# Three early loads of transposed x moved up the load queue, and the first scan's row copies issued by another engine

## The chip, the cores and the metric

The kernel runs on one core of one Trainium2 chip. The metric is the device time of one launch in microseconds (us); the time before is the median of three runs. The core has five engines that each work through a program of their own and wait for one another by semaphores: PE (TensorE, matmuls; PEld are its weight loads), DVE (VectorE), ACT (ScalarE), POOL (GpSimd) and SP (SyncE, which here issues every transfer). Transfers run on 16 DMA engines beside the compute engines.

## The reference, cut to what matters

Layer 0 is an attention over the 4096 pixels of each of four images, layer 1 a binarised 3x3 convolution with a batch norm.

```python
# x: (4, 256, 64, 64); K = 16
xf = x.reshape(B, C, N)                                   # N = 4096
f = einsum('kc,bcn->bkn', w1, xf) + b1[None, :, None]     # 16 features per pixel
energy = einsum('bkn,bkm->bnm', f, f)
attention = softmax(energy, axis=-1)
out = einsum('bcm,bnm->bcn', xf, attention)
x = x + out * 0.1
# layer 1
y = conv3x3(binary_act(x), alpha * sign(weights))
x = (y - mean(y)) * rsqrt(var(y) + eps) * gamma + beta + x
```

## The kernel before

**Tiling.** The attention goes over 32 chunks `t` of 512 columns (eight per image) and, in each, 16 steps `g`. A step makes one 128x1024 piece of energies on PE (line 401), its exponentials on ACT (line 508, tile P), a rounded copy on POOL (line 750, Ph), the remainder on DVE (line 610, Pl) and 24 matmuls on PE that multiply Ph and Pl with the halves xh and xl of the transposed x (line 428). Two steps ahead go the energies, and 24 steps ahead (`LAG`) a scan: it computes all energies of a chunk once in advance to find each row's maximum (DVE, line 600, tile nb) and the sum of its exponentials (ACT, line 519). All engines walk the same list `steps`, which begins 24 steps before the first attention step; `u = n + LAG` numbers the scan units from 0. The first 22 units are wide (128x1024, `scan_wide`, line 418) and go round three PSUM buffers in turn.

**The head.** Before the first scan unit, image 0 must give its features f. Eight pieces of x (512 KB each, `load_piece`, line 249) come in through six buffers; pieces 6 and 7 wait until the matmuls of `project(0)` have read pieces 0 and 1. `project(s)` (lines 392 to 395) turns two pieces into 1024 columns of f, ACT copies them out with the bias (`copy_f`, line 535), DVE splits them in a high and a low part (`split_f`, lines 585 and 593, tile hl). From hl, small copies inside the on-chip memory place the rows:

- `f_rows(s)` (line 272) makes four copies of 100 KB into T, first two for the scan (semaphore `ts_in`), then two for the energies (`te_in`).
- `scan_rows(t)` (line 290) makes three copies of 32 KB into U[t % 2] (semaphore `us_in`), the moving side of chunk t's scan; chunks 0 and 1 take their rows straight from hl[0].

The first scan unit waits for `us_in[0]` at 48 and for `ts_in[0]` at 32. `project(0)`, `(1)`, `(2)` stand ahead of unit 0 in PE's program, `project(3)` ahead of unit 4. On DVE, `split_f(0)` and `(1)` stand ahead of unit 0, `split_f(2)` ahead of unit 2 and `split_f(3)` ahead of unit 4. `split_f(2)` overwrites hl[0] and so waits for `us_in[0]`, `us_in[1]`, `ts_in[0]` and `te_in[0]` in front of line 593.

**The transposed x.** `load_xt(m)` (line 255) loads 512 KB of transposed x into one of three buffers (`XB = 3`, views of the tile wk). POOL makes xh and xl from it, two pairs of instructions for each load (`lower_x`, lines 741 and 743); image 0 has eight loads and so 16 pairs, and they stand ahead of the first `round_p` (line 750) in POOL's program. From the fourth load on, `load_xt` waits for the buffer.

**Order on SP.** All transfers are issued by SP in the order of its program: weights, pieces 0 to 5, pieces 6 and 7, `scan_rows(0)`, `f_rows(0)`, `scan_rows(1)`, then `f_rows(1)`, `load_xt(0)`, `f_rows(2)`, `load_xt(1)`, `f_rows(3)`, `load_xt(2)`, then `load_res(0)` (x for the final sum, line 262), and in the loop `energy_rows(0)` (line 297, a copy from U to U) and the loads 3 to 7 of the transposed x.

After the attention comes the convolution (lines 797 to 1062), which the change does not touch.

Of the kernel before, what the change touches and what calls it, by code (L numbers as in the profile page):

```python
# [6 lines left out]
F32 = mybir.dt.float32  # L7
# [11 lines left out]
KF = 16  # L19
KE = 3 * KF  # L20
KS = KE + 2
S0 = 64
# [14 lines left out]
FU = N // (2 * FW)  # L37
XP = 6
XB = 3
# [53 lines left out]
def attention(nc, x, xt, w1r, cols, wn, wt, rd, x2d, T0, shared):  # L93
# [5 lines left out]
    with ExitStack() as ctx:  # L99
# [10 lines left out]
        U = [sb(f"U{k}", [128, QC], F32R) for k in range(2)]  # L110
# [133 lines left out]
        def _(sp):  # L244
            def load_piece(s):
                if s >= XP:
                    sp.wait_ge(f_filled, 2 * ((s - XP) // 2 + 1))
                b, sl = divmod(s, SL)
                sp.dma_start(xp[s % XP], xb[b, :, :, sl * 512:(sl + 1) * 512]).then_inc(xp_in[s % XP], 16)

            def load_xt(m):
                if m >= XB:
                    sp.wait_ge(xl_done, 2 * (m - XB + 1))
                at = m * (4 * 128 * C)
                sp.dma_start(landed[m % XB].rearrange("p k c -> p (k c)"),
                             xt[at:at + 4 * 128 * C].rearrange("(p n) -> p n", p=128)).then_inc(xt_in[m % XB], 16)
# [18 lines left out]
            def scan_rows(t):  # L275
                b, q = divmod(t, CH)
                s = b * FU + q // 2
                if t < 2:
                    sp.wait_ge(hl_done, 1)
                else:  # L280
                    sp.wait_ge(ts_in[s % 2], 32 * (s // 2 + 1))
                if t >= 2:
                    sp.wait_ge(s_done, unit_count(SU * (t - 1) - 1))
                    sp.wait_ge(ue_in[t % 2], 16 * (t // 2))
                if t < 2:
                    src, row, s = hl[0], t * S0, slice(0, QC)
                else:
                    src, row, s = T[b % 2].bitcast(F32), S0, slice(q * QC, (q + 1) * QC)
                for to, at in ((0, 0), (1, 2), (2, 1)):
                    sp.dma_start(U[t % 2][S0 + to * KF:S0 + (to + 1) * KF, :].bitcast(F32),  # L290
                                 src[row + at * KF:row + (at + 1) * KF, s]).then_inc(us_in[t % 2], 16)
# [34 lines left out]
            sp.dma_start(col[:], cols).then_inc(col_in, 16)  # L326
            for s in range(2, XP):
                load_piece(s)
            for s in range(XP, SL):
                load_piece(s)  # L330
            scan_rows(0)
            f_rows(0)
            scan_rows(1)
            for s in range(1, FU):
                f_rows(s)
                load_xt(s - 1)
            load_res(0)
            for t in range(-1, NT):
                b, q = divmod(t, CH)
# [162 lines left out]
        @block.scalar  # L502
        def _(act):
            def exps(e):
                act.wait_ge(e_done, e + 1)
                if e >= 2:
                    act.wait_ge(pl_done, e - 1)
                mm = nc.scalar.activation(P[:, e % 2, :], ee[:], ACT.Exp)  # L508
                if e < PA:
                    mm.then_inc(p_done, 1)  # L510
                else:
                    act.wait_ge(av_done, 2 * (e - RP + 1))
                    nc.scalar.activation(Ph[:, e % RP, :], ee[:], ACT.Exp).then_inc(p_done, 1)  # L513

            def block_sum(v, to):
                t, j, i = unit_at(v)
                w = j * QT + i
                act.wait_ge(nmax_done, unit_count(v))
                nc.scalar.activation(to, to, ACT.Exp, bias=nb[:, t % 2, w:w + 1],  # L519
                                     accum_out=bsum[:, t % 2, w:w + 1]).then_inc(bsum_done, 1)  # L520

            def copy_bottom(t, c):
                if c == 0:
                    act.wait_ge(acc_done, 2 * (t + 1))
                else:
                    act.wait_ge(av_done, 2 * G * (t + 1))
                if t > 0:
                    act.wait_ge(x2_done, CT * (t - 1) + c + 1)
                nc.scalar.copy(tb[:, c, :], acc_b[c][:]).then_inc(bot_done, 1)  # L529

            def copy_f(s, bank):
                act.wait_ge(f_filled, 2 * (s + 1))
                if s >= 2:
                    act.wait_ge(hl_done, s - 1)
                nc.scalar.activation(Fp[s % 2][0:S0 + KS, :], bank[0:S0 + KS, 0:512], ACT.Identity,
                                     bias=col[0:S0 + KS, 0:1]).then_inc(fp_done, 1)

            act.wait_ge(fill_done, 1)
            nc.scalar.activation(dd[:, 0:1], sr[:, 31:32], ACT.Exp)
            act.wait_ge(col_in, 16)  # L540
            for t, g in steps:
                n = t * G + g
                e, u = n + 2, n + LAG
                for s in HEAD_F.get(u, ()):
                    copy_f(s, acc_t[s % 2])
                if g == 0 and t >= 1:
                    copy_bottom(t - 1, 1)
                if 0 <= e < NG:
                    exps(e)
                if u < UH:  # L550
                    block_sum(2 * u, wide[u % 3][:])
                elif u < NG:
                    block_sum(2 * u, sc[0])
                if g == G - 1 and 0 <= t < NT - 1:
                    copy_bottom(t, 0)
                if UH <= u < NG:
                    block_sum(2 * u + 1, sc[1])
                if g == 8 and 0 <= t + 1 < NT:
                    act.wait_ge(dd_done, t + 2)
                    nc.scalar.activation(wg[:], dd[:], ACT.Exp).then_inc(wg_done, 1)  # L560
                if projected(t, g) is not None:
                    copy_f(projected(t, g), ee)
                h = split_at(t, g)
                if h is not None:
                    m, p = divmod(h, 2)
                    b, k = divmod(h, 2 * XG)
                    act.wait_ge(xt_in[m % XB], 16 * (m // XB + 1))
                    act.wait_ge(av_done, 2 * ((b * CH - 1) * G + k + 1))
                    nc.scalar.copy(xh[:, 2 * k:2 * k + 2, :], landed[m % XB][:, 2 * p:2 * p + 2, :]).then_inc(xh_done, 1)
                if t == NT - 2 and g in (8, 10):  # L570
                    c = g // 2 - 4
                    act.wait_ge(w_in, 16 * CT)
                    nc.scalar.activation(sw[c].rearrange("p t o -> p (t o)"), xn[:, c, 0:TAPS * C],
                                         ACT.Sign).then_inc(w_signed, 1)
                if t == NT - 1 and 7 <= g < 11:
                    k, c = divmod(g - 7, CT)
                    act.wait_ge(pad_zero, 2)
                    sign_unit(nc, act, 0, k, xn, r0_in, 32, pads, signed, (c,))
# [543 lines left out]
```

## Time and profile before

| | |
|---|---|
| median of 3 runs | 1997.22 us (1996.63 to 1999.72) |
| the profiled execution | 1996.2 us, of which the span is 1994.3 us |
| PE busy | 1914.3 us, 96% of the span |
| DVE, ACT, POOL busy | 1618.3, 1419.3, 1200.6 us |
| mean granted clock of PE | 0.977 |

The span runs from the first to the last instruction of the profiled execution; 1.9 us of its time lie outside. "Busy" counts the time an engine works, and PEclk is the share of PE's full clock that was granted (0.50 is 1.2 GHz, 1.00 is 2.4 GHz). Times in the views are us from the start of the span unless marked ns.

### The profile page before, as it was taken

The numbers are of one execution on the slowest core, as the hardware profiler recorded it, in microseconds if no ns is written. First come the engines' busy times: TensorE is split into PE (matmuls) and PEld (weight loads), VectorE is DVE, ScalarE is ACT, GpSimd is POOL, SyncE is SP. The second block draws the span as 40 slices with busy tenths as digits, with TensorE's granted clock in tenths as the row PEclk, the third lists the DMA queues.
The fourth block names the chain that finished last, engine by engine and source line by source line (L and its number), as shares of the span: only waits on it lengthen the run. The fifth ranks groups of instructions, "written<-read, shape, count | busy, mean of one in ns | idle before, by whom it ended". The sixth has DMA issues, their size and how long they took to land. (4 is left out here: it accounts for less than half of the span.)

```text
span 1994.3 us, 40002 instructions
## 1 busy us (share of the span) xinstructions
PE 1914.3 (96%) x15232; PEld 1644.5 (82%) x15232; DVE 1618.3 (81%) x2151; ACT 1419.3 (71%) x2793; POOL 1200.6 (60%) x848
## 2 busy tenths in 40 slices
PE   6999999999999999999999999999999999989990
PEld 2789899998988899999899989998999999854440
DVE  5787888888888888888888888888888888777787
ACT  5777777778777777788777777788777777643335
POOL 4555555567755555567755556677655566477760
PEclk7899999999999999999999999999999999999995
DMA  6111111112211110122111110111011102433009
GB/s 213 40 50 61 53 38 35 31 64 67 81 40 50 59 40 32 32 72 95 53 60 57 40 40 23 56 57 53 32 32 32 32 30 77 170 145 120 1 35 387
DMA packets 58287, 133.67 MB, mean 67 GB/s; under 512 B 9328, under 2 KB 9328, under 8 KB 57584
## 3 DMA queue, kind: packets, MB, share of 16 engines
q1 hardware_dynamic: 58096, 131.10, 19.3%
q8 instruction: 122, 2.00, 0.4%
q14 instruction: 69, 0.57, 0.1%
HBM read 84.48 MB, written 33.62 MB: 59 GB/s over the span
## 5 line engine op out<-in xcount | busy, mean ns | idle before, releaser
L750 POOL CAST Ph<-P 128x1024 fp32r<-128x1024 f32 x496 | 722.6, 1457 | 641.4 <-ACT P L508 641.4
L519 ACT ACTIVATE scw<-scw,nb 128x512 f32<-128x512 f32 (+1 forms) x988 | 656.1, 664 | 345.4 <-DVE nb L600 345.2
L600 DVE TENSOR_REDUCE nb<-scw 128x1 f32<-128x512 f32 (+1 forms) x988 | 678.7, 689 | 255.7 <-PE scw L410 250.7
L428 PE MATMUL accb<-Ph,xh 64*128 64x512 f32 x2048 | 807.4, 394 | 1.3 <-ACT tb L529 1.3
L428 PE MATMUL acct<-Ph,xh 64*128 64x512 f32 x2048 | 807.4, 394 | 0.0
L428 PE MATMUL accb<-Ph,xl 64*128 64x512 f32 x2048 | 800.4, 391 | 0.0
L428 PE MATMUL acct<-Ph,xl 64*128 64x512 f32 x2048 | 796.5, 389 | 0.0
L610 DVE TENSOR_TENSOR Pl<-P,Ph 128x1024 fp32r<-128x1024 f32 x512 | 674.6, 1318 | 20.4 <-ACT Ph L513 15.9
L428 PE MATMUL acct<-Pl,xh 64*128 64x512 f32 x2048 | 635.4, 390 | 0.0
L428 PE MATMUL accb<-Pl,xh 64*128 64x512 f32 x2048 | 632.2, 388 | 0.0
L508 ACT ACTIVATE P<-ee 128x1024 f32<-128x1024 f32 x512 | 526.1, 1028 | 61.5 <-PE ee L401 39.7
L428 PEld LDWEIGHTS accb<-Ph,xh 64*128 64x128 f32 x2048 | 380.5, 186 | 26.8 <-issue 13.5
L410 PE MATMUL scw<-T,U 48*128 48x512 f32 x980 | 396.7, 405 | 4.0 <-ACT scw L519 1.8
L428 PEld LDWEIGHTS acct<-Ph,xl 64*128 64x128 f32 x2048 | 379.9, 186 | 17.2
L428 PEld LDWEIGHTS accb<-Ph,xl 64*128 64x128 f32 x2048 | 381.0, 186 | 15.2
L428 PEld LDWEIGHTS acct<-Ph,xh 64*128 64x128 f32 x2048 | 377.7, 184 | 15.7
L428 PEld LDWEIGHTS acct<-Pl,xh 64*128 64x128 f32 x2048 | 376.6, 184 | 17.0
L428 PEld LDWEIGHTS accb<-Pl,xh 64*128 64x128 f32 x2048 | 377.3, 184 | 12.5 <-DVE Pl L610 0.5
L401 PE MATMUL ee<-U,T 50*128 50x512 f32 x1024 | 327.1, 398 | 3.1 <-DMA U<-rows_t 1.9
L410 PEld LDWEIGHTS scw<-T,U 48*128 48x128 f32 x980 | 180.7, 185 | 35.6 <-ACT scw L519 27.6
L401 PEld LDWEIGHTS ee<-U,T 50*128 50x128 f32 x1024 | 190.1, 186 | 12.4 <-ACT accb L519 2.6
L519 ACT ACTIVATION_READ_ACCUMULATOR scw<-scw,nb 128x1 f32 x988 | 197.3, 200 | 0.0
(145 smaller groups left out, 1418.4 us busy)
## 6 DMA issues: line engine op xcount, KB each, us to landing
wk<-xt SPq DMA_DIRECT2D x32, 512.0 KB, 3.8
xres<-x SPq DMA_DIRECT2D x32, 512.0 KB, 3.9
x<-xres SPq DMA_DIRECT2D x32, 512.0 KB, 2.8
R<-rd SPq DMA_DIRECT2D x32, 256.0 KB, 3.1
xn<-x SPq DMA_DIRECT2D x16, 512.0 KB, 12.3
xr<-x SPq DMA_DIRECT2D x16, 512.0 KB, 9.9
out<-xr SPq DMA_DIRECT2D x16, 512.0 KB, 10.2
An<-x SPq DMA_DIRECT2D x14, 512.0 KB, 5.2
```

The lines of the kernel that those rows point to most:

```text
L401: return pe.matmul(ee[:, k * QC:(k + 1) * QC], T[b % 2][0:KS, m * 128:(m + 1) * 128], U[t % 2][0:KS, :], start=True, stop=True)
L410: pe.matmul(sc[v % 2], U[t % 2][S0:S0 + KE, i * 128:(i + 1) * 128], T[t // CH % 2][S0:S0 + KE, j * 512:(j + 1) * 512], start=True, stop=Tr ...
L428: return pe.matmul(to[:, :], w[rows, g * GM + k, c * 128:(c + 1) * 128], p[rows, s, k * QC:(k + 1) * QC], start=g == 0 and i == 0, stop=g ...
L508: mm = nc.scalar.activation(P[:, e % 2, :], ee[:], ACT.Exp)
L519: nc.scalar.activation(to, to, ACT.Exp, bias=nb[:, t % 2, w:w + 1], accum_out=bsum[:, t % 2, w:w + 1]).then_inc(bsum_done, 1)
L600: nc.vector.tensor_reduce(nb[:, t % 2, w:w + 1], of, AX.X, ALU.max, negate=True).then_inc(nmax_done, 1)
L610: nc.vector.tensor_tensor(Pl[:, e % RP, :], P[:, e % 2, :], Ph[:, e % RP, :].bitcast(F32), ALU.subtract).then_inc(pl_done, 1)
L750: nc.gpsimd.tensor_copy(Ph[:, e % RP, :], P[:, e % 2, :]).then_inc(ph_done, 1)
```

## The change

In SP's program, the loads 0 to 2 of the transposed x move up to right behind pieces 0 to 5, ahead of pieces 6 and 7. `f_rows(1)` moves ahead of `scan_rows(1)`. The three copies of `scan_rows(0)` leave SP; ACT issues the same three copies from its own queue, behind `copy_f(1)` and ahead of `copy_f(2)`, after a wait for the first `split_f`. The number of transfers, their sizes and what is computed stay the same.

```diff
@@ sync
             for s in range(2, XP):
                 load_piece(s)
+            for m in range(XB):
+                load_xt(m)
             for s in range(XP, SL):
                 load_piece(s)
-            scan_rows(0)
             f_rows(0)
+            f_rows(1)
             scan_rows(1)
-            for s in range(1, FU):
+            for s in range(2, FU):
                 f_rows(s)
-                load_xt(s - 1)
             load_res(0)
@@ scalar
+            def first_rows():
+                act.wait_ge(hl_done, 1)
+                for to, at in ((0, 0), (1, 2), (2, 1)):
+                    act.dma_start(U[0][S0 + to * KF:S0 + (to + 1) * KF, :].bitcast(F32),
+                                  hl[0][at * KF:(at + 1) * KF, :]).then_inc(us_in[0], 16)
+
@@ scalar, in the loop over steps
                 for s in HEAD_F.get(u, ()):
                     copy_f(s, acc_t[s % 2])
+                    if s == 1:
+                        first_rows()
```

## Rows read from the trace of the kernel before

**Rows 1.** The page's busy line of each engine (us, share of the span, instructions).

```profile
PE 1914.3 (96%) x15232; PEld 1644.5 (82%) x15232; DVE 1618.3 (81%) x2151; ACT 1419.3 (71%) x2793; POOL 1200.6 (60%) x848
```

**Rows 2.** Windows: stretch, length, PE, PEld, DVE, ACT, POOL busy, PEclk, DMA share, GB/s.

```profile
9.00:15.00 6.00, 5.28 (x20) 1.21 (x16) 2.36 (x4) 1.37 (x2) 0.00 (x0) 1.00 1.01 362
15.00:16.00 1.00, 0.10 (x2) 0.00 (x0) 0.00 (x0) 0.69 (x1) 0.00 (x0) 1.00 0.36 96
...
54.00:64.00 10.00, 8.28 (x23) 3.93 (x23) 5.47 (x7) 5.93 (x13) 7.23 (x8) 0.50 0.43 143
...
150.00:1700.00 1550.00, 1544.99 (x13081) 1416.23 (x13078) 1291.16 (x1735) 1193.75 (x2463) 961.48 (x689) 1.00 0.15 49
```

**Rows 3.** Timeline of SP's queue: start, length, line, operation, count.

```profile
4.26 0.47 SPq L249 DMA_DIRECT2D tab<-x  x1
10.44 0.88 SPq L249 DMA_DIRECT2D An<-x  x2
12.58 1.89 SPq L290 DMA_DIRECT2D U<-xn  x3
14.52 3.15 SPq L272 DMA_DIRECT2D T<-xn  x4
17.71 1.82 SPq L290 DMA_DIRECT2D U<-xn  x3
...
28.78 2.99 SPq L272 DMA_DIRECT2D T<-xn  x4
```

**Rows 4.** Timeline of the compute engines up to scan unit 4, same columns.

```profile
12.58 0.69 ACT L535 ACTIVATE xn<-acct,col 114x512 f32<-114x512 f32 x1 [1.38 <-PE acct L392]
...
15.14 0.69 ACT L535 ACTIVATE xn<-acct,col 114x512 f32<-114x512 f32 x1 [1.88 <-PE acct L392]
...
18.18 1.19 PE L418 MATMUL scw<-T,U 48*128 48x512 f32 x2 [3.08 <-DMA T<-xn]
...
22.12 0.75 DVE L593 SCALAR_TENSOR_TENSOR xn<-xn,col 114x512 fp32r<-114x512 f32 x1
...
27.54 0.43 DVE L585 CAST xn<-xn 114x512 fp32r<-114x512 f32 x1 [2.40 <-ACT xn L535]
```

**Rows 5.** Landing of the copies into T, us from issue.

```profile
DMA to landing us min/median/max: 2.7/2.8/3.0
```

**Rows 6.** DMA issues at 32.8 and at 54.7, the same copy: KB, us from issue to landing.

```profile
U<-U SPq DMA_DIRECT2D x1, 96.0 KB, 6.0
...
U<-U SPq DMA_DIRECT2D x1, 96.0 KB, 2.3
```

**Rows 7.** POOL's split of the transposed x: its two lines (ns) and what POOL waited for.

```profile
L741 POOL CAST xh<-wk x16: 611/620/709, 28.5 to 57.5; 128x512 fp32r<-128x512 f32 x16
L743 POOL TENSOR_TENSOR xl<-wk,xh x16: 1262/1272/1282, 29.3 to 58.2; 128x512 fp32r<-128x512 f32 x16
...
POOL xh L741 <- DMA wk<-xt: 27.7, 2, 27.5
```

**Rows 8.** Timeline at the first attention step, columns as in Rows 3.

```profile
55.96 1.02 ACT L508 ACTIVATE P<-ee 128x1024 f32<-128x1024 f32 x1 [0.91 <-PE ee L401]
...
58.53 0.69 DVE L600 TENSOR_REDUCE nb<-scw 128x1 f32<-128x512 f32 x1 [1.32 <-PE scw L410]
...
59.44 2.03 POOL L750 CAST Ph<-P 128x1024 fp32r<-128x1024 f32 x2
...
59.64 0.28 PEld L401 LDWEIGHTS ee<-U,T 50*128 50x128 f32 x1 [0.98 <-ACT P L508]
...
60.51 2.02 DVE L610 TENSOR_TENSOR Pl<-P,Ph 128x1024 fp32r<-128x1024 f32 x1 [1.29 <-POOL Ph L750]
...
62.59 0.28 PEld L428 LDWEIGHTS accb<-Pl,xh 64*128 64x128 f32 x1 [0.50 <-DVE Pl L610]
...
64.00 0.79 PE L410 MATMUL scw<-T,U 48*128 48x512 f32 x1 [0.19 <-ACT scw L519]
```

**Rows 9.** The row weights of a chunk on DVE, all 32 chunks (ns, min/median/max).

```profile
L653 DVE SCALAR_TENSOR_TENSOR wd<-wg,bsum x32: 174/741/1256, 46.9 to 1698.6; 128x32 f32<-128x32 f32 x32
```

## The prediction

> **What bounds the kernel now.** The busy line comes first: PE works for 96% of the span [rows 1], so it sets the time, and the first question is where its missing share lies. The windows answer it: between 150 and 1700 us PE is busy for 1544.99 of 1550 us, while from 54 to 64 us it reaches 8.28 of 10 at a granted clock of 0.50, its 1.2 GHz level [rows 2]. From the middle of the attention nothing is to be won, for the change puts no work there. What it can do is move the moment at which PE's unbroken work begins, at about 64 us; behind that moment every microsecond is handed on to the end one for one.
>
> So I read the head as a chain, from the timelines. DVE's first split is done just before 12.58, when SP begins to issue three copies into U and four into T [rows 3], and the first scan unit starts at 18.18 after PE has waited 3.08 us, last for T [rows 4]. T's second copy, which that unit needs, is issued at about 15.3 (the four take 3.15 us) and lands 2.8 us later [rows 5], at 18.1: it fits. From there 22 wide units run round PE, DVE and ACT up to the first exponentials at 55.96 [rows 8]. A second chain meets it there: POOL's 16 pairs on the transposed x start at 28.5, because their load comes late [rows 7], and end just before 59.44, when POOL can first round P, though P was ready at 56.98 [rows 8].
>
> **The change part by part.**
>
> *The three loads moved up.* They are issued from about 4.8 on, right behind the last of six pieces [rows 3], so nothing ahead of them changes and the work on pieces 0 to 5 stays where it is. But they fill the DMA engines for 3 x 524 KB / 362 GB/s = 4.35 us, at the rate of a stretch in which the engines are full (share 1.01) [rows 2]. Today they drain at about 15.2, shortly after 15 (share 0.36 from 15 to 16) [rows 2]; with the loads, at about 19.5. POOL has their first at about 14.6, where the six pieces and 512 KB more are through. The question is whether a small copy issued later waits for that. The same row copy from U to U takes 2.3 us with an empty queue and 6.0 us with two 512 KB loads issued in front of it [rows 6]: 3.7 us more, and two loads at 362 GB/s are 2.9 us. So a copy on SP's queue waits for what stands ahead of it.
>
> That decides T. Its first two copies are issued 1.94 us earlier (12.58 instead of 14.52 [rows 3]), but stand behind loads that drain at 19.5. Two copies of 100 KB at 362 GB/s are 0.6 us, and some tenths go to the landing: 20.4. The first scan unit starts at about 20.4 instead of 18.18, **+2.2 us**. Bounds: nothing waits, then T lands at 12.58 + 0.8 + 2.8 = 16.2, the copies into U decide, and the unit starts at 17.3 to 17.8, -0.4 to -0.9 us; or the whole 4.35 us come through. I take +2.2, since rows 6 show the wait and the difference between full queue and empty one by row.
>
> *The copies into U by ACT.* No row shows ACT issuing a transfer. By SP's rate they take 1.89 us for three [rows 3]; from the end of `copy_f(1)` at 13.27 that is 15.16, and `copy_f(2)`, now at 15.14 [rows 4], starts 0.0 later. At twice the price it is 1.9 us later, at no price it is not earlier, for it waits for PE. Both are covered: what it makes is not read on DVE until just ahead of 22.12 [rows 4]. Without that cover ACT would hold up its first exponential. The third copy's issue begins at 14.5 and by rows 5, the nearest for such a copy, it lands at 17.2 to 17.5, ahead of T.
>
> The Trainium skill, page "DMA: Bandwidth & Descriptors", section "Issuing engines are not separate DMA queues", speaks against a gain here: a transfer begun by another engine runs on the same 16 DMA engines and only the issuing engine's time is saved. Its section "Queues, rings and completion order" adds that each engine takes one ring's descriptors in order and goes round between SP's and ACT's rings, so that U's copies could pass the loads and T's could not. By that, T still decides at 20.4, the sum stays, and the chance of the first rival falls; rows 6 agree for SP's ring, and no row shows ACT's.
>
> *`f_rows(1)` ahead of `scan_rows(1)`.* The copies into U[1] leave SP at about 18.8 to 20.7 instead of 17.71 to 19.53 [rows 3] and, behind eight copies into T, land at about 23. DVE waits for them in `split_f(2)`, in front of line 593, with the maxima of units 2 and 3 queued behind it. It comes there at 22.12 + 2.2 = 24.3 [rows 4]: no wait. Should there be one, the first 2.4 us are free, because DVE idles as long before `split_f(3)`, waiting for PE and ACT [rows 4].
>
> *Pieces 6 and 7* land by 19.5; `project(3)`, which reads them, stands behind unit 3 and so behind 20.4: free.
>
> *Where POOL's chain goes.* POOL starts at about 14.6 and is through with three loads at 26, 13.9 us earlier. But the fourth load stands in SP's program behind `f_rows(3)`, which waits for `split_f(3)`: 28.78 + 2.2 + 2.99 = 33.97 [rows 3], the load itself at about 35.0, landing at about 40.2 (5.2 us: 2.3 empty and two loads of 1.45). So POOL idles from 26 to 40, then does ten pairs at (59.44 - 28.5) / 16 = 1.93 us [rows 7, 8]: free at 59.5. P is ready at 56.98 + 2.2 = 59.2. POOL's lateness shrinks from 2.5 us to 0.3.
>
> *What that is worth.* Less than it looks. PE does not wait for Ph today: its energies of step 2 begin only at 59.64, released by ACT, and stand ahead of the first attention matmul. It loses 0.5 us at 62.59 waiting for Pl and some tenths before 64.00, where a scan waits for ACT, and ACT in turn for the maxima queued on DVE behind `Pl` [rows 8]. That instruction started 1.3 us late and took 2.02 us beside POOL's casts. With the head 2.2 us later, DVE's maximum ends at 61.4, Pl runs 61.4 to 62.6, as early as today, and PE goes through without the stop: **-0.5 us**, between 0 and -1.4.
>
> Sum: +2.2 - 0.5 = **+1.7 us**, on the profiled 1996.2 us: 1997.9. The median of the three runs is 1.0 us above the profiled execution, so I forecast 1997.22 + 1.7 = **1998.9 us**, +0.09%. A measurement of this kernel can tell about 0.2%, that is 4.0 us, from no change; this is inside.
>
> **The rivals.**
>
> *The small copies don't wait (head earlier).* For it: SP is rid of 1.89 us of issuing ahead of T, and POOL is early. Against it: rows 6. Then the first unit starts 0.4 to 0.9 us earlier, POOL is free at about 56.5 and PE's stop goes as well: -0.7 - 0.5 to -1.4, together about -1.7 us: 1995.5.
>
> *The queue hands on all of its delay (slower).* The mechanism is the same wait at full price: if the copies into T land after 22.5, the first unit is 4.35 us late. For it: those copies may meet an engine that drains last, and rows 6 show 0.8 us more than two loads explain. Against it: they are issued 1.94 us earlier, and today they reach an almost empty queue with 2.8 us of their own, part of which now passes while they queue. With it POOL ends no earlier relative to P, and DVE's row weights, 0.17 to 1.26 us long as they meet POOL or not [rows 9], may add 0.5: 1997.22 + 4.35 + 0.5 - 0.5 = 2001.6, +0.2%. It decides against the kernel from +4.0 us.
>
> *The change does little:* queue and earlier issue cancel, within 0.5 us of 1997.2.
>
> **How the numbers follow.** Forecast 0.53, first rival 0.27, second 0.12 (of which 0.09 beyond 4.0 us), third 0.08. Faster by over 0.2% would need more than the first rival gives; I leave 0.03 of its chance for a gain that I don't see. So faster 0.03, within 0.2% 0.88, slower 0.09. The range reaches from the first rival's far end (-0.9 - 1.4 = -2.3, to 1994.9) to the second (2001.6).
>
> **What would show it.** The first scan unit at about 20.4, its wait ended by T; POOL's first cast at about 14.6 and a gap of some 14 us after its sixth pair; `split_f(2)` without a wait; `copy_f(2)` at 15.2; POOL's first rounding right behind P; no wait of PE for Pl. The forecast is wrong if the first unit starts at 18 or earlier (copies pass the loads), if it waits for U (ACT's queue is slow to start), or if the head ends more than 4 us away from 64.0. From there on the two traces should run in parallel to the end.

## The result and the profile after

The changed kernel takes 2000.65 us (median of 19 runs, 1998.07 to 2002.08) where the kernel before takes 1996.81 (19 runs beside them): a ratio of 1.0019 [1.0012, 1.0026], +3.84 us. The forecast was +1.7, within 0.2%. The profiled execution took 2001.38 us with a span of 1999.5; before it was 1996.2 and 1994.3. The profiled pair lies 5.2 us apart and the medians 3.84, because one profile fell above its median and the other below. The working that follows goes by the profiled pair.

The page's busy line (us, share of the span, instructions) answers [rows 1]: PE has 0.5 us more, POOL 1.4 us less, so nothing was added to any engine. The 5.2 us are idle time.

```profile
PE 1914.8 (96%) x15232; PEld 1653.1 (83%) x15232; DVE 1618.3 (81%) x2151; ACT 1418.1 (71%) x2793; POOL 1199.2 (60%) x848
```

The windows say where it isn't: from 150 to 1700 us the stretch is the same as in [rows 2]. From 9 to 15 the DMA engines move 409 GB/s, more than before, and from 15 to 19 they are still full (share 1.05 and 1.00) where before their share had fallen to 0.42 and 0.48 (columns as in [rows 2]).

```profile
9.00:15.00 6.00, 4.82 (x20) 1.15 (x16) 2.36 (x4) 1.37 (x2) 0.53 (x1) 1.00 1.04 409
15.00:17.00 2.00, 0.21 (x2) 0.00 (x0) 0.00 (x0) 0.69 (x1) 1.89 (x3) 1.00 1.05 389
17.00:19.00 2.00, 0.00 (x0) 0.00 (x0) 0.00 (x0) 0.00 (x0) 1.87 (x3) 1.00 1.00 289
19.00:21.00 2.00, 0.00 (x0) 0.00 (x0) 0.00 (x0) 0.00 (x0) 1.92 (x3) 0.72 0.74 158
...
150.00:1700.00 1550.00, 1545.07 (x13082) 1424.08 (x13081) 1292.48 (x1733) 1192.19 (x2467) 958.29 (x688) 1.00 0.15 49
```

The timeline of the changed kernel, over the same steps as [rows 3, 4, 7, 8], with its columns:

```profile
12.34 6.20 SPq L272 DMA_DIRECT2D T<-xn  x8
...
12.58 1.90 ACTq L542 DMA_DIRECT2D U<-xn  x3
...
14.47 0.61 POOL L750 CAST xh<-wk 128x512 fp32r<-128x512 f32 x1 [13.44 <-DMA wk<-xt]
...
15.25 0.69 ACT L536 ACTIVATE xn<-acct,col 114x512 f32<-114x512 f32 x1 [2.00 <-PE acct L393]
...
22.84 1.19 PE L419 MATMUL scw<-T,U 48*128 48x512 f32 x2 [7.63 <-DMA T<-xn]
...
43.89 0.61 POOL L750 CAST xh<-wk 128x512 fp32r<-128x512 f32 x1 [17.98 <-DMA wk<-xt]
...
48.54 1.15 DVE L653 CAST sh<-negm 128x4 fp32r<-128x4 f32 x1
...
52.30 1.24 DVE L662 SCALAR_TENSOR_TENSOR wd<-wg,bsum 128x32 f32<-128x32 f32 x1 [0.26 <-ACT wg L569]
53.47 0.60 DVE L667 COPY sr<-sh 128x4 f32<-128x4 f32 x1
...
61.37 1.02 ACT L509 ACTIVATE P<-ee 128x1024 f32<-128x1024 f32 x1 [0.92 <-PE ee L402]
...
62.93 1.03 POOL L759 CAST Ph<-P 128x1024 fp32r<-128x1024 f32 x1
...
64.55 1.22 DVE L619 TENSOR_TENSOR Pl<-P,Ph 128x1024 fp32r<-128x1024 f32 x1
...
68.87 0.62 PE L411 MATMUL scw<-T,U 48*128 48x512 f32 x1
...
71.51 0.40 PE L411 MATMUL scw<-T,U 48*128 48x512 f32 x1
```

The last of these steps in the kernel before:

```profile
66.33 0.40 PE L410 MATMUL scw<-T,U 48*128 48x512 f32 x1
```

Four differences against the kernel before carry the result. The first scan unit starts at 22.84 instead of 18.18 [rows 4], **+4.66 us**, and waits 7.63 us for T instead of 3.08. The first exponential comes 38.53 us behind that unit instead of 37.78 (55.96 - 18.18 [rows 4, 8]), **+0.75**; together +5.41 at 61.37. From there to PE's first scan of the attention, 68.87 against 64.00 [rows 8], the lag is +4.87: **-0.54**, for DVE's `Pl` takes 1.22 us instead of 2.02 and PE no longer waits for it. At the next scan, 71.51 against 66.33, the lag is +5.18: **+0.31**. The granted clock rises from 0.50 to 1.00 at 65.3 in the kernel before and at 71.1 here, so PE works on at the 1.2 GHz level for 2.2 us behind the mark instead of 1.3, and more than half of what it won at `Pl` is lost again. The end of the span is 5.2 us later.

The DMA issues of the changed kernel. Columns: operation, count, KB, us from issue to landing, for pieces 6 and 7 of x and the first and the third of the copies into U that ACT issues, each in its own window of issue.

```profile
An<-x SPq DMA_DIRECT2D x1, 512.0 KB, 8.8
...
An<-x SPq DMA_DIRECT2D x1, 512.0 KB, 11.1
...
U<-xn ACTq DMA_DIRECT2D x1, 32.0 KB, 5.3
...
U<-xn ACTq DMA_DIRECT2D x1, 32.0 KB, 6.6
```

Piece 7, the last of the loads, is issued at 10.6 and has landed at 21.7; in the kernel before it was issued at 10.9, took 5.5 and had landed at 16.4. The loads therefore end 5.4 us later, not the 4.35 of the prediction. By the trace's records of each landing, T is complete at 22.7, 1.0 us behind piece 7. ACT's three copies have landed at 17.9, 18.8 and 20.4: behind the loads of the transposed x (17.0), but the first two ahead of piece 6 (19.1) and all three ahead of piece 7, which were issued before them.

### The profile page after: what moved, and what is told of

It reads as the page before. It is cut to its first block and busy times, and to the rows that moved or that the text cites. A ratio compares the mean times of both kernels' runs of the same rounds, so it can differ in the third digit from the quotient of the medians.

```text
span 1999.5 us, 40002 instructions
## 1 busy us (share of the span) xinstructions
PE 1914.8 (96%) x15232; PEld 1653.1 (83%) x15232; DVE 1618.3 (81%) x2151; ACT 1418.1 (71%) x2793; POOL 1199.2 (60%) x848
## 3 DMA queue, kind: packets, MB, share of 16 engines
q1 hardware_dynamic: 58000, 131.01, 19.1%
## 5 line engine op out<-in xcount | busy, mean ns | idle before, releaser
L619 DVE TENSOR_TENSOR Pl<-P,Ph 128x1024 fp32r<-128x1024 f32 x512 | 673.8, 1316 | 19.1 <-ACT Ph L514 15.9
```

What stands on the lines that cost most here:

```text
L619: nc.vector.tensor_tensor(Pl[:, e % RP, :], P[:, e % 2, :], Ph[:, e % RP, :].bitcast(F32), ALU.subtract).then_inc(pl_done, 1)
```

## The experiments

Two theories, with their rivals. **Q, the queue:** a row copy into T or U ends only when the loads ahead of it have passed on the same DMA engines; the three loads moved up are the whole of the +4.66. Its rivals: the order of the row copies costs it, ACT's queue costs it, or the copies are slow in themselves. **P, the port:** what the first exponential loses behind the first unit is DVE's short instructions on SBUF, which stand still until POOL's current instruction of the split is over; the rival is PE, ACT or a wait of the 22 units. Times given as "first unit" and "first exponential" are the starts of the lines at 22.84 and 61.37 above, in each kernel's timeline. The edits are shown against the changed kernel, but those of "The three loads alone", of the first narrowed split and of the last two versions against the kernel before.

Each kernel left one trace, and a first unit is not the same in every execution: kernels whose transfers up to it are the same start it at 18.18 and 18.72 (before, and the version that holds POOL), and at 18.19 and 18.99 (the rows alone, and the late loads). A difference of up to 0.8 us between two first units therefore shows nothing by itself.

### The two parts of the change one by one

The three loads alone, everything else as before:

```diff
+            for m in range(XB):
+                load_xt(m)
             for s in range(XP, SL):
                 load_piece(s)
...
             for s in range(1, FU):
                 f_rows(s)
-                load_xt(s - 1)
```

> The kernel before with nothing but the three loads of transposed x moved up behind pieces 0 to 5; all row copies stay on SP in the old order. Theory Q (the copies into T wait in SP's queue until the loads in front of them are through): the first scan unit starts at 22.5 to 23.5 us instead of 18.18, and the time is 3 to 5 us above before. Theory R (the delay comes from the new issue of the row copies, ACT's queue or f_rows(1) directly behind f_rows(0)): the first scan unit starts at 18 to 18.5 and the time is within 1 us of before, or below it by what POOL's earlier start gives back (0.5 us).

Measured: 2000.25 us against 1996.85 for the kernel before, ratio 1.0019 [1.001, 1.0028]. Timeline of this kernel:

```profile
22.03 1.20 PE L419 MATMUL scw<-T,U 48*128 48x512 f32 x2 [6.61 <-DMA U<-xn]
...
59.48 1.02 ACT L509 ACTIVATE P<-ee 128x1024 f32<-128x1024 f32 x1 [0.92 <-PE ee L402]
```

By the medians the loads alone cost as much as the whole change. U ends the wait here, although U's copies are issued ahead of T's. The first unit starts 0.8 us before that of the changed kernel, no more than such marks differ by themselves, and the profiled execution is a short one (1999.25 us).

The rows alone, the loads where they were before:

```diff
-            for m in range(XB):
-                load_xt(m)
...
             f_rows(1)
             scan_rows(1)
+            load_xt(0)
             for s in range(2, FU):
                 f_rows(s)
+                load_xt(s - 1)
```

> The changed kernel with the three loads of transposed x back where they were, between the f_rows; ACT's copies into U and f_rows(1) ahead of scan_rows(1) stay. Theory Q: the first scan unit starts at 17.3 to 17.9 us, and the time is 0 to 1.5 us below before. Theory R: the first scan unit starts at 21 to 23 us and the time is 3 to 5 us above before.

Measured: 1998.28 us, ratio 1.0005 [0.9996, 1.0014]: not told apart from no change. Timeline:

```profile
18.19 1.22 PE L419 MATMUL scw<-T,U 48*128 48x512 f32 x2 [3.32 <-DMA U<-xn]
...
27.59 1.47 DVE L594 CAST xn<-xn 114x512 fp32r<-114x512 f32 x1 [2.17 <-ACT xn L536]
...
44.95 1.00 DVE L653 CAST sh<-negm 128x4 fp32r<-128x4 f32 x1
```

The first unit starts at 18.19, as before, although T's copies are issued first: now U is last. Putting T's copies first gives nothing while the others run beside pieces 6 and 7.

One load moved up instead of three:

```diff
-            for m in range(XB):
-                load_xt(m)
+            load_xt(0)
...
             for s in range(2, FU):
                 f_rows(s)
+                load_xt(s - 1)
```

> The changed kernel with one load (512 KB) moved up instead of three; the other two go between the f_rows as before the change. Theory Q: each load taken out of the queue gives back 1.45 to 1.6 us, so the first scan unit starts at 19.6 to 20.0 us instead of 22.84. Theory R: the row copies are the same as in the changed kernel, so it starts at 22 to 23 us.

Measured: 1998.43 us in a single run. Timeline:

```profile
19.24 0.73 PE L419 MATMUL scw<-T,U 48*128 48x512 f32 x2 [3.97 <-DMA U<-xn]
```

With none, one and three loads in front the first unit starts at 18.19, 19.24 and 22.84: 1.05 us for the first load, 1.80 for each of the other two. The dose tells that the loads decide. It doesn't tell whether a load costs more than its 1.45 us at 362 GB/s: the five kernels with three loads in front start at 22.0 to 23.6, the five with none (and the rows behind the pieces) at 18.2 to 19.0, 4.2 us apart on the mean, against 4.35.

### Rows ahead of the last loads, and loads behind the rows

The row copies ahead of pieces 6 and 7, the transposed x late:

```diff
+            f_rows(0)
+            scan_rows(1)
             for s in range(XP, SL):
                 load_piece(s)
-            f_rows(0)
             f_rows(1)
-            scan_rows(1)
-            for s in range(2, FU):
-                f_rows(s)
+            f_rows(2)
+            load_xt(0)
+            f_rows(3)
+            load_xt(1)
+            load_xt(2)
```

> The changed kernel with the order on SP turned round: f_rows(0) and scan_rows(1) go ahead of pieces 6 and 7, and the loads of transposed x go last (the first behind f_rows(2), the others behind f_rows(3)). Theory Q (row copies wait for the loads in front of them): with nothing but pieces 0 to 5 in front, the first scan unit starts at 16.6 to 17.2 us (18.18 before, 22.84 after the change). If theory P holds too (a cast on DVE stands still while POOL works on the transposed x), POOL, which then starts at about 28, leaves the cast of split_f(3) at 0.43 us, and the first exponential comes at 54.0 to 55.3 us (55.96 before); the time is 0.5 to 2 us below before. Rival: the head has another limit (project(3), or the copies into U[1]) that takes the gain back before the first exponential; then it comes at 55.5 to 56.5.

Measured: 2002.9 us against 1997.13, ratio 1.003 [1.0018, 1.0042], slower than the changed kernel by the medians (the intervals of the two ratios overlap a little). Timeline:

```profile
17.01 0.72 PE L420 MATMUL scw<-T,U 48*128 48x512 f32 x2 [1.42 <-DMA U<-xn]
...
28.09 0.43 DVE L595 CAST xn<-xn 114x512 fp32r<-114x512 f32 x1 [4.57 <-ACT xn L537]
...
64.89 2.02 DVE L620 TENSOR_TENSOR Pl<-P,Ph 128x1024 fp32r<-128x1024 f32 x1 [3.51 <-POOL Ph L760]
```

With no load beside them ACT's copies land 2.5 us after their issue, and the first unit starts 1.2 us earlier than before: the gain that the first rival spoke of is there, at the price of pieces 6 and 7. They are issued at 17.68, and `split_f(3)` waits 4.57 us instead of 2.40; by unit 6 the lead is gone (28.26 against 28.21 before). The first exponential comes at 58.11, not at the 54.0 to 55.3 that I expected, although the cast of `split_f(3)` takes 0.43 us. The second loss is POOL's: it starts at 29.37 and reaches the first P only at 63.82, though P was ready at 59.13, and DVE waits 3.51 us for it. A third one is the same in the next version and is told there.

The same late loads, with pieces 6 and 7 ahead of the rows:

```diff
-            for m in range(XB):
-                load_xt(m)
...
-            for s in range(2, FU):
-                f_rows(s)
+            f_rows(2)
+            load_xt(0)
+            f_rows(3)
+            load_xt(1)
+            load_xt(2)
```

> The kernel of e2 with the loads of transposed x one place later on SP (the first behind f_rows(2), the others behind f_rows(3)), so that POOL starts at 28 us instead of 24.9. In e2 the first scan unit started as early as before (18.19) but the first exponential came 1.67 us later. Theory P (DVE's casts stand still while POOL works): the cast of split_f(3) falls from 1.47 back to 0.43 us and the first exponential comes at 55.9 to 56.9 us instead of 57.63. Rival: the 1.67 us come from the late copies into U[0] and U[1] and stay: 57.3 to 58.

Measured: 2003.1 us, ratio 1.003 [1.0018, 1.0041]. Timeline:

```profile
28.39 0.43 DVE L595 CAST xn<-xn 114x512 fp32r<-114x512 f32 x1 [2.40 <-ACT xn L537]
...
52.91 2.70 SPq L302 DMA_DIRECT2D U<-rows_t  x4
...
56.80 0.76 PE L403 MATMUL ee<-U,T 50*128 50x512 f32 x1 [3.81 <-DMA U<-rows_t]
...
64.91 2.02 DVE L620 TENSOR_TENSOR Pl<-P,Ph 128x1024 fp32r<-128x1024 f32 x1 [3.62 <-POOL Ph L760]
```

The first unit starts at 18.99 and the first exponential at 58.03, 3.3 us ahead of the changed kernel, and the kernel is nonetheless slower than it. POOL starts at 30.88 here, stands idle for 2.5 us more until its next load, and reaches the first P at 63.84: DVE waits 3.62 us for `Ph`. The head has two ends: an early start of the first unit, and POOL's sixteen pairs ready when the first P is. Before, with POOL's start at 28.5 and its first P at 59.44, DVE waits 1.29 us for it already [rows 7, 8]; 4.4 us more of lateness put the end there.

The cast of `split_f(3)` fell to 0.43 us as theory P said, but the first exponential came at 58.03 instead of 55.9 to 56.9, and P is not the reason: by the sum of the table below the interval would be 37.57 us, and it is 39.04. DVE has the row statistics (rows_t) at 51.05, but SP issues their copy into U only at 52.91: ahead of it stands the eighth load of the transposed x, issued at 52.53, which waits for a buffer that the late POOL frees at 52.5. PE's first energies wait 3.81 us for that copy; in the changed kernel they wait 1.92. Behind the head the granted clock rises only at 73.5 (65.3 before), and the lag grows from 4.4 us at PE's first scan of the attention to 6.1 at the ninth exponential of the attention (89.24 against 83.10).

### The price of POOL beside DVE

The split narrowed to 8 of 256 columns, in the order of before:

```diff
+            nc.gpsimd.memset(xh[:].bitcast(F32), 0.0).then_inc(fill_done, 1)
+            nc.gpsimd.memset(xl[:].bitcast(F32), 0.0).then_inc(fill_done, 1)
...
-                    nc.gpsimd.tensor_copy(xh[:, tiles, :], landed[m % XB][:, 2 * p:2 * p + 2, :])
+                    nc.gpsimd.tensor_copy(xh[:, tiles, 0:8], landed[m % XB][:, 2 * p:2 * p + 2, 0:8])
```

> The kernel before, but POOL's split of the transposed x of image 0 is left out (xh and xl are zeroed at the start and only 8 of 256 columns are made), so POOL is idle from the middle of the head on. Theory P: the three short DVE instructions of the first row statistics, 0.40, 1.26 and 0.61 us long before, fall to about 0.15, 0.17 and 0.06, and the first exponential comes at 53.8 to 54.4 us instead of 55.96, though the first scan unit starts where it did (18.0 to 18.4). Rival (their length has another reason): they stay, and the first exponential comes at 55.5 to 56.2.

Measured: 1998.8 us in a single run. Timeline:

```profile
7.82 6.92 POOL L736 MEMSET xl<- 128x8192 f32 x1
...
11.04 3.98 DVE L585 CAST xn<-xn 114x512 fp32r<-114x512 f32 x1 [11.04 <-ACT xn L535]
...
21.43 1.19 PE L418 MATMUL scw<-T,U 48*128 48x512 f32 x2 [5.94 <-DMA T<-xn]
...
47.13 0.17 DVE L644 CAST sh<-negm 128x4 fp32r<-128x4 f32 x1
...
49.92 0.19 DVE L653 SCALAR_TENSOR_TENSOR wd<-wg,bsum 128x32 f32<-128x32 f32 x1 [0.26 <-ACT wg L560]
50.03 0.16 DVE L658 COPY sr<-sh 128x4 f32<-128x4 f32 x1
...
57.48 1.02 ACT L508 ACTIVATE P<-ee 128x1024 f32<-128x1024 f32 x1 [0.91 <-PE ee L401]
```

The total tells nothing on P, and the marks that I had forecast (18.0 to 18.4, and 53.8 to 54.4) were missed, for the filling that was added runs on POOL at the start and held DVE's first cast back: the rows are issued at 15.84 instead of 12.58. That cast is itself the plainest sight of P: it takes 3.98 us instead of 0.43 and ends at 15.02, 0.28 us behind the end of POOL's fill at 14.74. The interval tells the rest: 57.48 - 21.43 = 36.05 us, where before it is 37.78.

The same narrowing, with the same two fills, in the changed kernel:

```diff
+            nc.gpsimd.memset(xh[:].bitcast(F32), 0.0).then_inc(fill_done, 1)
+            nc.gpsimd.memset(xl[:].bitcast(F32), 0.0).then_inc(fill_done, 1)
...
-                    nc.gpsimd.tensor_copy(xh[:, tiles, :], landed[m % XB][:, 2 * p:2 * p + 2, :])
+                    nc.gpsimd.tensor_copy(xh[:, tiles, 0:8], landed[m % XB][:, 2 * p:2 * p + 2, 0:8])
```

> The changed kernel with POOL's split of image 0 left out as in e7. Theory Q and P together: the first scan unit starts at 22.5 to 23.1 us as in the changed kernel, and the first exponential comes 4.4 to 4.9 us behind that of e7, at 58.4 to 59.2 us (61.37 with the split): the queue's part alone, without POOL's. Rival (the delay beyond the queue's is not POOL's): 5.2 to 5.6 us behind that of e7.

Measured: 2000.13 us in a single run. Timeline:

```profile
15.84 6.20 SPq L272 DMA_DIRECT2D T<-xn  x8
...
22.23 1.22 PE L419 MATMUL scw<-T,U 48*128 48x512 f32 x2 [6.96 <-DMA U<-xn]
...
58.30 1.02 ACT L509 ACTIVATE P<-ee 128x1024 f32<-128x1024 f32 x1 [0.91 <-PE ee L402]
```

The interval is 36.07 us: without POOL's split both orders need the same time from first unit to first exponential, so the 0.75 us between them are POOL's. A rival for them was PE's clock, which is granted at 0.50 through that whole interval in the changed kernel and at 1.00 from 27.8 to 31.2 in the kernel before. These two runs rule it out: the first narrowed split has such a stretch at 1.00 too (30.3 to 33.7), this one has none, and their intervals are 0.02 us apart. And because of the fills this run is the sharpest one on Q: T's copies are issued 3.5 us later than in the changed kernel (15.84, not 12.34), and the first unit starts no later (22.23 against 22.84). When a copy was issued didn't matter here while the loads ahead of it were still under way.

What the instructions lose beside POOL adds up to the interval. Excess is each kernel's duration less that of the narrowed kernel (CAST `sh` 0.17, `wd` 0.19, COPY `sr` 0.16, the CAST of `split_f(3)` 0.43), and forecast is 36.06 + excess; the durations are from the timelines of the kernels.

| kernel | sh | wd | sr | other | excess | forecast | measured |
|---|---|---|---|---|---|---|---|
| before | 0.40 | 1.26 | 0.61 | | 1.75 | 37.81 | 37.78 |
| changed | 1.15 | 1.24 | 0.60 | | 2.47 | 38.53 | 38.53 |
| loads alone | 0.65 | 0.66 | 0.61 | | 1.40 | 37.46 | 37.45 |
| rows alone | 1.00 | 1.24 | 0.61 | `split_f(3)` 1.47 | 3.37 | 39.43 | 39.44 |
| one load | 0.69 | 1.26 | 0.61 | | 2.04 | 38.10 | 37.53 |

The row of one load is 0.57 us off: its first unit took 0.73 us instead of 1.19 (the line above; the granted clock is 1.00, the 2.4 GHz level, from 19 to 20, where in the kernel before it is 0.50 at the first unit), which is 0.46 of it. For the versions with 48 rows and with T's copies by ACT (below) the same sum gives 37.56 and 37.40, and 37.62 and 37.19 were measured; the rows first, the late loads and the pieces behind T have a further wait in the interval. The Trainium skill, page "SBUF — State Buffer", section "SBUF: two separate sides", says that VectorE and GpSimd share one pair of ports as an exclusive lock, held for a whole instruction by whichever took it first; of VectorE's instructions it names those in a two-port mode and those with two inputs in SBUF. The trace agrees in size: 0.17 us becomes 1.15 beside POOL's instruction of 1.27 us at 48.39, and a cast of 0.43 us lasts until the fill's end. That it is this lock, and which forms of DVE's instructions come under it, no run here shows.

### Round the queue

Fewer rows in the scan copies of the changed kernel, 48 instead of 50. The trace's records of landings show each copy of 50 rows ended by 10 of the 16 engines and each of 48 rows by all 16:

```diff
+                        rows = KE if base else KS
-                        sp.dma_start(T[b % 2][base:base + KS, at:at + 512].bitcast(F32),
-                                     hl[s % 2][j * S0:j * S0 + KS, :])
+                        sp.dma_start(T[b % 2][base:base + rows, at:at + 512].bitcast(F32),
+                                     hl[s % 2][j * S0:j * S0 + rows, :])
```

> The changed kernel, but the two copies of each f_rows that the scan reads carry 48 rows instead of 50 (the two rows that only the energies read are left out there, nothing reads them). It asks whether the copies into T are slow by themselves once their turn has come. Theory S (they are: 8 copies of 100 KB move at some 160 GB/s and fewer rows spread better over the DMA engines): the first scan unit starts at 21.2 to 21.8 us instead of 22.84. Theory Q (they wait for the slowest engine to finish the loads): 22.3 to 22.9.

Measured: 2000.41 us in a single run, the first unit at 23.16 with 7.73 us of wait for T. That is no earlier than with 50 rows (22.84), where the spread over the engines should have given 1.0 to 1.6 us: the spread isn't the price, and the place behind the loads is what is left.

The first two copies into T issued by ACT too, and left out on SP:

```diff
+                    if s == 0 and base == S0:
+                        continue
...
             act.wait_ge(hl_done, 1)
+            for j in range(2):
+                act.dma_start(T[0][S0:S0 + KS, j * 512:(j + 1) * 512].bitcast(F32),
+                              hl[0][j * S0:j * S0 + KS, :]).then_inc(ts_in[0], 16)
             for to, at in ((0, 0), (1, 2), (2, 1)):
```

> The changed kernel, but ACT issues f_rows(0)'s two scan copies into T as well, ahead of its three into U; SP keeps the loads early and the other copies. It asks whether what T waits for is its place in SP's queue or the busy DMA engines. Theory Q (the place in SP's queue): T now goes round the loads like U's copies did (those took 5.3 to 6.6 us from issue in the changed kernel); the first two leave ACT at about 12.6 to 14.1 and land at 18 to 20, U's three leave by 16 and land at 20 to 21.5; the first scan unit starts at 20 to 21.5 us instead of 22.84. Rival (the engines take old transfers first whichever queue a copy comes from): 22.3 to 23.3.

Measured: 2000.99 us in a single run. Timeline:

```profile
23.58 1.22 PE L421 MATMUL scw<-T,U 48*128 48x512 f32 x2 [8.08 <-DMA U<-xn]
```

By the trace's records of each landing T was complete at 21.2 instead of 22.7, and U at 23.5 by the last copy. U's copies now stand behind T's on ACT's queue, so what T won U lost. Q as I had put it, that SP's queue is what holds the copies, said 20 to 21.5 and is wrong there: ACT's queue is held up nearly as long. The Trainium skill, page "DMA: Bandwidth & Descriptors", section "Issuing engines are not separate DMA queues", says that it is the same 16 engines whoever issues; the trace agrees, with 5.3 to 6.6 us for ACT's copies of 32 KB in the changed kernel and 2.5 with no load beside them.

Pieces 6 and 7 behind the first rows of T in the changed kernel, so that three loads stand ahead of T instead of five:

```diff
             for m in range(XB):
                 load_xt(m)
+            f_rows(0)
             for s in range(XP, SL):
                 load_piece(s)
-            f_rows(0)
             f_rows(1)
```

> The changed kernel with pieces 6 and 7 issued behind f_rows(0): the three loads of transposed x stay early, but T waits for 1 MB less. Theory Q: the first scan unit starts 2.9 to 3.6 us earlier than in the changed kernel, at 19.2 to 20.0 us, and project(3), which reads pieces 6 and 7, is not late by more than 1 us behind unit 3. Rival (only the loads of transposed x hold T up, for their rows are twice as long): 22 to 23.

Measured: 2002.7 us in a single run. Timeline, and windows of the same kernel:

```profile
22.28 1.22 PE L419 MATMUL scw<-T,U 48*128 48x512 f32 x2 [5.92 <-DMA U<-xn]
...
27.77 0.75 DVE L602 SCALAR_TENSOR_TENSOR xn<-xn,col 114x512 fp32r<-114x512 f32 x1 [1.55 <-DMA U<-xn]
```

```profile
17.00:19.00 2.00, 0.00 (x0) 0.00 (x0) 0.00 (x0) 0.10 (x1) 1.92 (x3) 1.00 1.01 230
19.00:21.00 2.00, 0.00 (x0) 0.00 (x0) 0.00 (x0) 0.00 (x0) 1.92 (x3) 0.77 1.06 268
```

I had expected a first unit at 19.2 to 20; it came at 22.28, U last (T was complete at 21.2, U at 22.2). Two things in the trace speak to the miss. The engines are full (share 1.01 and 1.06) but move 230 and 268 GB/s, where stretches with hardly a row copy in them move 362 [rows 2] to 409: with row copies among the loads, both take longer than their bytes say. And one of the 16 engines ran behind the others: 15 engines had finished the third load of the transposed x by 18.8, the last at 19.5, and a transfer has landed only with its last engine. Why that engine lags isn't settled, nor is how much of the miss is due to each of the two.

### A version without the early loads

If P is right, the time lies in keeping POOL off DVE's row weights, and the loads can stay where they were. POOL waits with its pairs 8 and 9 until the row weights are done, and does the last six between its first roundings of P. On SP the last of the eight loads moves behind the copies of the row statistics:

```diff
-                    if t == -1 and g in (2, 4, 6, 8, 10):
+                    if t == -1 and g in (2, 4, 6, 8):
...
+                    if t == -1 and g == 12:
+                        load_xt(XG - 1)
...
-            for h in range(2 * XG):
+            for h in range(8):
                 lower_x(h)
+            pool.wait_ge(row_done, 1)
+            for h in range(8, 10):
+                lower_x(h)
...
                     round_p(e)
+                if 0 <= e < 2 * XG - 10:
+                    lower_x(10 + e)
```

> The kernel before, with its transfers as they were, but POOL holds its split of the transposed x after 8 of 16 pairs until DVE has the first row statistics, does two more pairs, and does the last six one by one behind the first roundings of P; the last of the eight loads moves behind the copies that carry the row statistics. Theory P (short DVE instructions stand still while POOL works; they cost 1.75 us before the first exponential, and POOL's lateness another 0.5 us behind it): the three instructions fall to 0.17, 0.19 and 0.16 us, the first exponential comes at 54.0 to 54.5 us instead of 55.96, PE does not wait for Pl, and the time is 1.5 to 3 us below before. Rival: the pairs that now stand beside the first attention steps hold up Pl and take it back; the time is within 1 us of before.

Measured: 1995.53 us against 1996.94, ratio 0.9993 [0.9984, 1.0002]. Timeline:

```profile
18.72 0.70 PE L420 MATMUL scw<-T,U 48*128 48x512 f32 x2 [3.11 <-DMA T<-xn]
...
47.63 0.19 DVE L655 SCALAR_TENSOR_TENSOR wd<-wg,bsum 128x32 f32<-128x32 f32 x1 [0.26 <-ACT wg L562]
...
55.19 1.02 ACT L510 ACTIVATE P<-ee 128x1024 f32<-128x1024 f32 x1 [0.92 <-PE ee L403]
...
58.37 1.92 DVE L612 TENSOR_TENSOR Pl<-P,Ph 128x1024 fp32r<-128x1024 f32 x1
...
62.70 0.62 PE L412 MATMUL scw<-T,U 48*128 48x512 f32 x1
```

`wd` takes 0.19 us instead of 1.26 [rows 9], PE's first attention scan comes 1.3 us earlier than before (62.70 against 64.00), and DVE waits no more for `Ph`. The median is 1.4 us under that of the kernel before; this measurement doesn't tell that from no change, but its interval and that of the changed kernel don't meet. CAST `sh` is still 1.09 us: pair 7 lies beside it. With that and a later first unit (18.72) the first exponential misses the 54.0 to 54.5 that I expected. The lead at the first scan doesn't last in the profiled execution: its span is 1994.8 us, 0.5 us longer than before. The granted clock rises at 65.3 in both kernels, so that the lead is 0.8 us at the next scan (65.51 against 66.33), and behind the attention the clock stays at 0.50 for 6.8 us (from 1772.0) where in the trace of before it does so for 3.4 (from 1775.4).

The same with the first two scan copies into T ahead of those into U:

```diff
-            scan_rows(0)
-            f_rows(0)
+            f_rows(0, 0)
+            scan_rows(0)
+            f_rows(0, 1)
             scan_rows(1)
```

> e11, and on SP the two scan copies of f_rows(0) go ahead of the three copies into U (the two energy copies stay behind them). Theory Q: with T's copies issued 1.9 us earlier and U's 1.5 us later, in front of a queue that holds only pieces 6 and 7, the first scan unit starts at 17.3 to 18.0 us instead of 18.18; with P, the first exponential at 53.2 to 54.2 us and the time 2 to 3.5 us below before. Rival: U's copies are then the late ones by as much, and the first scan unit stays at 18.1 to 18.5.

Measured: 1996.15 us, ratio 0.9996 [0.9987, 1.0005]. Timeline:

```profile
18.77 1.22 PE L422 MATMUL scw<-T,U 48*128 48x512 f32 x2 [3.39 <-DMA U<-xn]
```

The first unit doesn't start earlier than in the version above, nor than before: U is last then, as with the rows alone, and the first exponential (55.22, expected 53.2 to 54.2) and the time miss the forecast. Two runs (this and that one) say the same: at the kernel's old place an early start needs the whole group of row copies, and which of them is first doesn't matter.

## Why the prediction was right, and where its size was off

The verdict (within 0.2%), the sign and the place were right: the time stays in the head, the first scan unit waits for T, T waits for the loads, and from the next stage on the traces run nearly in parallel (5.2 us apart at the ninth exponential of the attention, 4.8 at its last one, 5.2 at the end). The size was not: +3.84 us by the medians and +5.2 in the profiled pair, for +1.7. What happened in the queue is the second rival's case, which had a chance of 0.12, and not the forecast's with 0.53; that both lie within 0.2% is what makes the verdict right, and so it is in part luck. By one of the prediction's own signs the forecast was wrong: the head ends at 68.87, more than 4 us away from 64.0. Of its terms:

- **The queue, +2.2 forecast, +4.66 measured.** This is the term that was mis-sized, and two readings in it failed. "Today they drain at about 15.2" was read from the mean share of 16 engines (0.36 from 15 to 16 [rows 2]); but a transfer has landed when its last engine is through, and piece 7 had landed at 16.4: 1.2 us. And "fill the DMA engines for 4.35 us" took the rate of loads alone (362 GB/s), where row copies run among the loads: the loads ended 5.4 us later, at 21.7, with 289 and 158 GB/s in the last stretches: 1.0 us, which is within what such marks differ from trace to trace (21.2 to 22.6 in the five traces with three loads in front). The step behind them, 0.9 us from the end of the loads to T, was right: 22.7 - 21.7 = 1.0. The second rival had the mechanism at full price and its point of decision, T after 22.5: that case occurred. Its sum (4.35 + 0.5 - 0.5, +0.2%) is near what the trace shows, term by term: 4.66, 0.72 by the table, -0.54.
- **The landing of T's copies, 2.8 us [rows 5]:** the line of rows 5 belongs to three copies from T into U, issued from 44.7 on, and not to copies into T. The landing records of the kernel before put T's second copy, issued at 15.44, at 18.04, 2.6 us later, so that the mistake cost nothing.
- **POOL beside DVE: not in the sum, +0.72.** The prediction counted POOL's earlier start as a gain at P alone. The rows of DVE's weights [rows 9] showed the row weights at 0.17 to 1.26 us, and it was used for the second rival only; the first chunk's own cost, 1.75 us, stood in the trace of before, and an early POOL changed which instructions it hits: `sh` went from 0.40 to 1.15.
- **PE's stop at the attention, -0.5 forecast, -0.54 measured**, by the mechanism given: `Pl` alone on DVE takes 1.22 us, as early after the maximum as forecast. The prediction then hands every microsecond on one for one; the later rise of the granted clock took 0.31 of it back, a term that it did not have.
- **POOL's chain:** first cast at 14.47 (14.6 forecast), but the gap is 17.98 us, not 14, as the fourth load comes behind a later `f_rows(3)`; POOL reaches P 0.54 us after it is ready, not 0.3.
- **ACT's issues:** 1.90 us (1.89) and `copy_f(2)` at 15.25 (15.16): right, and hidden. That U lands at 17.2 to 17.5 was wrong: 5.3 to 6.6 us from issue instead of 2.8 took it to 20.4. It cost nothing here, since T was later still; with the loads alone and with T's copies by ACT, U is what PE waits for.
- **`split_f(2)` and `project(3)` without a wait:** right; in the version with pieces 6 and 7 behind the rows `split_f(2)` did wait, 1.55 us.
- **The first rival** (the copies don't wait) is refuted by the loads alone and by one load; the gain that it priced appears only where no load is under way (17.01). Copies on ACT's queue did pass pieces 6 and 7, as the prediction allowed, but not the loads of the transposed x, and T's copies on SP's queue landed behind all of them.

## What to carry to other kernels

A load that is moved ahead to use idle DMA time is paid by the small copies behind it, here with nearly its whole time; read when its last engine lands, not when the mean share falls. Before an off-path engine is started earlier, look at what it will run beside: here POOL's split beside DVE's row weights cost as much as the stop that it took away. An engine that starts later has a price too: it holds its buffers longer, and with them the issuing engine and every copy behind the load that waits. An interval between two marks on the path, taken with the suspect removed, tells more than the total, which moved for other reasons.

## What the runs showed of the hardware

Three short DVE instructions of the first chunk (`sh`, `wd`, `sr`) took 0.16 to 0.19 us alone and up to 1.26 beside POOL's, about the length of POOL's current instruction; a cast of 0.43 us took 3.98 beside a fill of 6.92. Four of the five intervals in the table follow from the sum of such losses to 0.03 us. With row copies among the loads the DMA engines were full (share 1.00 to 1.06) at 230 to 289 GB/s; with hardly a row copy among them the loads reached 362 to 409. T's copies, moved from SP's queue to ACT's, were complete 1.5 us earlier (21.2 for 22.7, one trace each). One of 16 engines was 0.7 us behind the other 15 at the end of a run of loads (19.5 for 18.8), and the landing waited for it; its cause is open.
